# Layer norm sums and scales moved to a PSUM bank in the attention-score stage of a four-layer graph network

## The reference, cut to what matters

```python
xh = (h @ gat_w).reshape(n, H, C)
a_src = jnp.sum(xh * att_src, axis=-1)          # attention scores of the sources
e = _leaky(a_src[s2] + a_dst[d2], NEG_GAT)
...
e_t = _mlp2(edge_attr, W1e, b1e, W2e, b2e)      # layer 2: factors of the edges
out = x + aggregated * res_w                    # layer 2: nodes without an edge have aggregated = 0
mu = jnp.mean(out, axis=-1, keepdims=True)
var = jnp.mean(jnp.square(out - mu), axis=-1, keepdims=True)
return (out - mu) * jax.lax.rsqrt(var + EPS) * gamma + beta
```

## Time and profile before

| what | value |
| --- | --- |
| median of 3 runs | 5640.13 us |
| lowest and highest run | 5633.73 and 5650.66 us |
| span of the profiled execution, which is also its own time here | 5641.0 us |
| VectorE busy in the span | 4168.8 us, 74% |
| GpSimd busy in the span | 3788.1 us, 67% |
| TensorE busy in the span | 3732.6 us, 66% |
| ScalarE busy in the span | 2361.1 us, 42% |

### The profile page before, as it was taken

One profiled execution on the slowest core, in us unless ns is written; L12 is line 12 of the kernel. 1 busy time (PEld: TensorE's weight loads), 2 busy tenths in 40 slices (PEclk: granted clock), 3 DMA queues, 4 the chain that ended last, 5 costly groups with the idle time before them and its releaser, 6 DMA issues. The chain is left out here.

```text
span 5641.0 us, 69641 instructions
## 1 busy us (share of the span) xinstructions
PE 3732.6 (66%) x15267; PEld 1851.4 (33%) x15267; DVE 4168.8 (74%) x6266; ACT 2361.1 (42%) x4957; POOL 3788.1 (67%) x3734
## 2 busy tenths in 40 slices
PE   8997788847776999677727876777555546552110
PEld 3443555533332333244414442333222212221000
DVE  8876789957774555788868988999655559996442
ACT  0000678833331222466618973343222247772221
POOL 7776766767775777577724337666377767774777
PEclk9998899977876555788869998899766568885555
DMA  5533987744442222455524433333244423332221
GB/s 59 77 53 56 153 203 226 234 136 107 107 106 55 61 63 61 141 182 171 181 64 129 137 117 76 82 83 82 79 130 131 131 69 76 76 73 65 68 72 51
DMA packets 538641, 595.34 MB, mean 106 GB/s; under 512 B 300576, under 2 KB 315046, under 8 KB 536923
## 3 DMA queue, kind: packets, MB, share of 16 engines
q1 hardware_dynamic: 319004, 473.91, 28.7%
q0 software_dynamic: 115712, 91.82, 9.1%
q10 hardware_dynamic: 103840, 28.71, 4.2%
HBM read 354.69 MB, written 303.31 MB: 117 GB/s over the span
## 5 line engine op out<-in xcount | busy, mean ns | idle before, releaser
L1135 POOL DMA_INDIRECT l_got<-d_x,l_near x1176 | 1157.6, 984 | 557.5 <-issue 354.6
L1135 POOL DMA_INDIRECT p_got<-d_h,p_near x392 | 440.2, 1123 | 155.8 <-issue 118.9
L848 PE MATMUL ps<-hot_lo,hot_w 128*128 128x512 bf16 x2352 | 510.0, 380 | 13.4 <-DVE hot_lo L785 13.4
L1135 POOL DMA_INDIRECT p_got<-d_sums,p_near x392 | 401.4, 1024 | 151.7 <-issue 149.3
L2457 POOL DMA_INDIRECT out<-fi_res,fi_near x392 | 381.0, 972 | 181.1 <-issue 118.2
L726 POOL DMA_INDIRECT d_pos<-place,near x392 | 400.2, 1021 | 125.2 <-issue 119.1
L1135 POOL DMA_INDIRECT p_got<-d_ext,p_near x392 | 382.2, 975 | 132.4 <-issue 117.1
L1143 POOL DMA_INDIRECT ln_xd<-d_xt,idsE x304 | 286.9, 944 | 136.8 <-issue 96.9
L2131 PE MATMUL ps<-l_hid,w2n 128*64 128x512 f32 x392 | 234.8, 756 | 162.2 <-DVE l_sums L1308 155.7
L412 PE MATMUL ps<-ident,fi_sums 64*128 64x64 f32 x392 | 53.1, 314 | 424.8 <-DVE fi_sums L1308 424.8
L848 PEld LDWEIGHTS ps<-hot_lo,hot_w 128*128 128x128 bf16 x2352 | 230.6, 98 | 293.2 <-issue 17.3
(11 more groups left out here) (391 smaller groups left out, 10871.3 us busy)
## 6 DMA issues: line engine op xcount, KB each, us to landing
l_xd<-d_x SPq DMA_DIRECT2D x147, 256.0 KB
d_ext<-ln_ext SPq DMA_DIRECT2D x98, 264.0 KB
d_xt<-in_x_wide ACTq DMA_DIRECT2D x49, 520.0 KB
ln_x<-in_x SPq DMA_DIRECT2D x98, 256.0 KB
d_h<-ln_hb SPq DMA_DIRECT2D x98, 256.0 KB, 2.9
d_x<-ln_x SPq DMA_DIRECT2D x98, 256.0 KB
lb_x<-d_x SPq DMA_DIRECT2D x49, 512.0 KB
d_x<-lb_x SPq DMA_DIRECT2D x49, 512.0 KB
```

The costliest lines, as they stand in the source:

```text
L848: last = nc.tensor.matmul(bank(h), hot_w[:, r, k], hot_lo[:, r, 512 * h:512 * h + 512], start=False, stop=False)
L1135: nc.gpsimd.indirect_dma_start(out=out[:, q], out_offset=None, in_=source, in_offset=bass.IndirectOffsetOnAxis(ap=ids[:, q:q + 1], axis=0) ...
```

## The change

The norm of the stage gets bank 1 as `small`: `norm.sum` is then columns 0 to 15 and `norm.gain` columns 16 to 31 of that bank. The scores, which had bank 1, are written to the first eight partitions of bank 0, where the transposed rows lay. Two waits of TensorE change with it: `scores` no longer waits for the copy of the scores before, and `turned` waits for that copy in place of the copy `hf` of the group before.

```diff
-        norm = NormLagged(sem, t, "lb", WIDE)
+        norm = NormLagged(sem, t, "lb", WIDE, bank(1))
...
                 def scores(i, r, g):
                     yield 2
                     hold(pe, m["hf_done"], g + 1)
-                    hold(pe, m["att_done"], g)
-                    nc.tensor.matmul(bank(1)[0:2 * HEADS], W.att_half[:].rearrange("k q h -> k (q h)"), hf[:, r % 2],
+                    nc.tensor.matmul(bank(0)[0:2 * HEADS], W.att_half[:].rearrange("k q h -> k (q h)"), hf[:, r % 2],
                                      start=True, stop=True).then_inc(m["mm"], 1)
 
                 def turned(i, r, g):
                     yield 5
                     hold(pe, landed[r], i * 128 + 128)
-                    hold(pe, m["hf_done"], g)
+                    hold(pe, m["att_done"], g)
                     transpose_pairs(nc, bank(0), got[:, r], W).then_inc(m["got_t"], 1)
...
-                    nc.scalar.activation(att[:, r % 2], bank(1)[0:2 * HEADS], ACT.Copy).then_inc(m["att_done"], 1)
+                    nc.scalar.activation(att[:, r % 2], bank(0)[0:2 * HEADS], ACT.Copy).then_inc(m["att_done"], 1)
```

## The result

The changed kernel takes 5581.6 us in the median of 4 runs (5574.0 to 5587.2), the kernel before, with one more run beside it, 5637.8 (5633.7 to 5650.7). The ratio is 0.9895, with a 95% interval from 0.9882 to 0.9908. That is 56 us less; 5580 was forecast.

The account below looks back on a forecast made before the run. GpSimd's back-to-back gathers were taken as the bound. Freed holds of 64.9 us less 4.0 of new ones gave 60.9, so 5641.0 - 60.9 = 5580.1 us, about 5580 as a median, range 5568 to 5608.

Parts of the forecast that it names:

- What bounds: In the changed stage GpSimd issues gathers back to back, 11.44 us a group; VectorE needs 9.16 and has time to spare.
- Centring and scaling read PSUM: Lines 341 and 1606 keep one SBUF input each and stop holding gathers: 35.7 + 29.2 = 64.9 us off GpSimd.
- What takes their place: Line 1619, still with two SBUF inputs, holds gathers by chance: 6.1 us for 49 groups, 4.0 more than before.
- GpSimd's pace: GpSimd's gathers in the stage take 10.10 us a group, a gain of 60.9 us.
- Is anything else late: VectorE's added PSUM time is hidden at 9.2 us a group; the stage's tail, index loads and DMA cost nothing.
- Scores in bank 0: TensorE's transposes newly wait for the copy of the scores, a wait always met already; cost 0.
- A: Rival: gathers are not freed, the hold coming from something other than the second SBUF input; 5640 us, chance 0.06.
- C: Rival: the copy of the scores delays TensorE's transposes; at 11 us a group 44 us slower, 5684 us, chance 0.03.

Follow-up runs that it names:

- The runs with row sums: The changed kernel with one more VectorE row sum per group: over 128 columns 5592.2 us, ratio 0.9891 to before; over 256 columns 5592.5 us, ratio 0.9911.
- the scales alone with the row sum: The changed kernel with the norm's sums back in SBUF, only its scales in PSUM, plus a 128-column VectorE row sum per group; 5607.7 us, ratio 0.9940 to before.
- the scales alone: The changed kernel with the norm's sums back in SBUF, so only its scales lie in PSUM; 5615.4 us, ratio 0.9914 to before.

## Why the prediction was right, and where it was not

- **What bounds.** Right. GpSimd fills the stretch before and after, and every run's stage follows its holds: from the first gather to the first of group 48, 549 us with 70 of holds, 499 with 18, 484 with 3.5.
- **Centring and scaling read PSUM.** Right, and now shown for each by itself. The Trainium skill says the same in "SBUF — State Buffer", section "Who interferes with whom", of a VectorE instruction with two SBUF inputs against a GpSimd instruction that reads SBUF; its other inference, that tensor_tensor does not stall such a DMA, does not hold for these gathers, which line 1606, a tensor_tensor, held by up to 0.8 us before the change.
- **What takes their place.** Wrong, and this is the step that failed. I priced line 1619 at 0.124 us a group "with no fixed phase to VectorE", because 8 x 1.247 and VectorE's step "have no common measure". They need none: a held gather takes its phase from the instruction that held it. The holds were 14.9 us, not 6.1, so 12.8 more than before in place of 4.0. The right question was whether VectorE's step lies between seven gathers (8.73 us) and seven gathers plus the longest hold (9.29); 9.20 does. The runs with row sums show that the same question has to be put for two steps and fifteen gathers (18.71 to 19.26 us). The adding of 35.7 and 29.2 us had the same fault. It came out right for the sum only because both instructions went at once.
- **GpSimd's pace.** Forecast 10.10 us a group; measured 498.7 / 48 = 10.39. The 60.9 us of gain in the stage were 50.7: 8.8 of what is missing are the leaky instruction's holds, 1.1 the late indices. That the total of 5580 was met within 2 us is luck. In the profiled run the stage began 10.8 us early, which the change did not cause; beside later runs the changed kernel was 52 us (5602.8 to 5654.9) and 49 us (5591.3 to 5640.7) under before, near the 50.7 that the stage gives.
- **Is anything else late.** Right for VectorE: its step stayed at 9.20, the sums cost 8 ns and the scales 6 ns more per group. The last result came 24.0 us after its group's first gather, 24.1 before. I costed index loads at nothing; they cost 1.1 us, in one wait.
- **Scores in bank 0.** Cost 0, as said: 1.0001 by itself. After the change TensorE's transposes of gathered rows wait 26 times, 39.8 us, and each time for the rows to land, never for the copy of the scores. Rivals A and C fall with the runs above.

## What to carry to other kernels

Where GpSimd issues indirect DMAs back to back, look at the spread of their durations: if the median is low and some are much longer, find what VectorE executes at their starts. Move the smallest of two SBUF operands of such an instruction to PSUM, or let it read the PSUM product directly. A hold couples the two loops. So do not add such holds up or spread them by chance when one loop meets another: compare the steps of the two loops, over one step and over two. What is left between a whole number of gathers and VectorE's step sets the loss, and not how long VectorE could hold.

## What the runs showed of the hardware

A gather is sensitive only at its start. One that was running when line 1606 began took 0.94 us, and VectorE's instruction 1.22, so neither waited for the other; one that began within it was held until its end less 0.13 us. In all the traces, once the masks are done, no gather is held by more than 0.03 us unless it begins inside an instruction with two SBUF inputs. The start works the other way too. In the scales alone with the row sum a gather begins 0.05 us after line 341, is not held, and line 341 takes 1.30 us in place of 1.23:

```profile
2784.59 1.30 DVE L341 SCALAR_TENSOR_TENSOR lb_four<-lb_sum,lb_x 128x1024 f32<-128x1024 f32 x1
2784.64 0.94 POOL L1135 DMA_INDIRECT p_got<-d_h,p_near  x1 [0.30 <-issue]
```

A hold can also run through several instructions. The kernel before has such a gather in gated_messages, where three centrings with two SBUF inputs follow each other:

```profile
3711.81 0.68 DVE L177 SCALAR_TENSOR_TENSOR l_s_xc<-l_s_sum,l_got 128x512 f32<-128x512 f32 x1
3711.87 2.65 POOL L1135 DMA_INDIRECT l_got<-d_x,l_near  x1 [0.30 <-issue]
3712.41 0.68 DVE L177 SCALAR_TENSOR_TENSOR l_d_xc<-l_d_sum,l_xd 128x512 f32<-128x512 f32 x1
3713.01 0.69 DVE L177 SCALAR_TENSOR_TENSOR l_o_xc<-l_o_sum,l_o 128x512 f32<-128x512 f32 x1
```

It is held for 1.70 us, to the end of the third less 0.13. In the stage of the change it is otherwise: line 1619 follows line 341 just as closely, and yet with the scales alone the gather at 2380.58 is let go when line 341 ends. No run shows what makes the difference. In gated_messages such holds add up to 33 us of gathers; the change leaves them, and no run shows what they cost there.

And more work on an engine that is not the bound can shorten a stage: 14.1 us of row sums on VectorE removed 12.2 us of holds on GpSimd, while with the centring still able to hold for up to 1.1 us the same work added 5.4.
